# A state-space layer with its feed-forward block on eight cores: two kinds of diagonal weights sent through the weight ring, dt's row spread by DMA, one LayerNorm placed a stage earlier

## The reference

```python
xc, z = split(x @ W_in.T)                       # 2 x 2048 channels
xc = silu(causal_conv4(xc) + conv_b)            # each channel alone, 4 taps
dt, B, C = one, 16 and 16 rows of xc @ W_x.T
delta = softplus(dt * w_dt + b_dt)              # per channel
h_t = exp(delta_t * A) * h_(t-1) + delta_t * xc_t * B_t      # 16 states per channel
y = (sum over states of h_t * C_t) + D * xc
x1 = LayerNorm(x + (y * silu(z)) @ W_out.T)
h = gelu(x1 @ W1.T + scale * (rank-16 terms from 16 tokens) + b1)
x2 = LayerNorm(x1 + h @ W2.T + scale * (rank-16 terms) + b2)
```

## Time and profile before

| | |
|---|---|
| median of 3 runs | 3696.67 us (3695.38 to 3697.18) |
| the profiled execution | 3725.95 us |
| its span, core 3 (the slowest) | 3724.2 us |
| spans of the cores | 3678.0 to 3724.2 us |
| VectorE busy | 3136.2 us (84%) |
| TensorE busy | 3208.1 us (86%) |
| GpSimd busy | 1099.5 us (30%) |

### The profile page before, as it was taken

How to read it: one execution, slowest core, us unless ns; L and a number is a source line. 1 busy time by engine, 2 the same in 40 slices (tenths; PEclk the granted TensorE clock), 3 DMA queues, 4 the chain that set the end, 5 groups by cost and what they waited for, 6 DMA issues and landing times.

```text
span 3724.2 us, 72456 instructions; the slowest of 8 cores (3678.0 to 3724.2 us)
## 1 busy us (share of the span) xinstructions
PE 3208.1 (86%) x21816; PEld 2116.9 (57%) x21816; DVE 3136.2 (84%) x2688; ACT 2825.6 (76%) x4263; POOL 1099.5 (30%) x1541
## 2 busy tenths in 40 slices
PE   6666677988999889998999889998899879899998
PEld 2333344655666556655666556665566546666676
DVE  1999999988998999989988999999998899898400
ACT  4777768887797978878797977979788877977322
POOL 6222332224322143123323143332342242221312
PEclk9788888999999999999999989999999989988787
DMA  7466874435554444444554444544444435544565
GB/s 123 64 88 98 131 148 108 137 108 151 151 146 132 120 145 142 144 121 120 164 146 128 125 142 134 151 125 131 151 148 132 123 109 156 148 128 123 169 196 172
DMA packets 272053, 500.76 MB, mean 134 GB/s; under 512 B 28208, under 2 KB 67504, under 8 KB 270256
## 3 DMA queue, kind: packets, MB, share of 16 engines
q1 hardware_dynamic: 240320, 407.96, 37.2%
q0 software_dynamic: 14464, 71.26, 11.8%
q10 hardware_dynamic: 16896, 16.91, 1.3%
HBM read 533.59 MB, written 55.18 MB: 158 GB/s over the span
## 4 chain that ended last, share of the span: by engine, by line
PE 51%; DVE 21%; issue 13%; ACT 11%; POOL 2%; DMA 1%; DVEq 1%; ACTq 0%; SPq 0%; POOLq 0%
DVE hq L1030 14%; PE ps_f L696 8%; PE ps_dbx L546 8%; PE ps_f L732 8%; PE ps_y L562 8%; PE ps_f L574 7%; DVE hm L1040 6%; PE ps_f L638 4%; ACT da L876 3%; ACT L876 2%; PE ps_f L585 2%; PE ps_f L708 1%; ACT hh L935 1%; DVE xy L1047 1%; PE ps_f L719 1%
## 5 line engine op out<-in xcount | busy, mean ns | idle before, releaser
L1030 DVE TENSOR_TENSOR_SCAN hq<-da,state,ps_dbx 128x512 bf16<-128x512 f16 x1536 | 1856.5, 1261 | 216.6 <-PE ps_dbx L546 163.1
L876 ACT ACTIVATE da<-delta,prm_sb 128x512 f16<-128x512 f32 x2048 | 1363.0, 714 | 186.6 <-DVE hq L1030 128.1
L546 PE MATMUL ps_dbx<-dp,vt 128*128 128x256 bf16 x4096 | 649.5, 284 | 306.2 <-DVE hq L1030 303.0
L1030 DVE TENSOR_TENSOR_SCAN hq<-da,ps_dbx 128x512 bf16<-128x512 f16 x512 | 587.5, 1201 | 137.5 <-PE ps_dbx L546 121.9
L1040 DVE TENSOR_TENSOR hm<-hq,crep 128x2048 bf16<-128x2048 bf16 x512 | 698.4, 1364 | 2.3 <-PE ps_y L562 1.8
L546 PEld LDWEIGHTS ps_dbx<-dp,vt 128*128 128x128 bf16 x4096 | 385.7, 101 | 528.1 <-issue 428.1
L562 PE MATMUL ps_y<-hm,cst_sb 128*128 128x512 bf16 x2048 | 582.4, 411 | 0.7 <-DVE hm L1040 0.7
L1159 POOL CAST state<-hq 128x4 f32<-128x4 bf16 x384 | 71.8, 187 | 1701.1 <-DVE hm L1040 1696.4
L574 PE MATMUL ps_f<-xT,wr 128*128 128x512 bf16 x2048 | 498.7, 388 | 54.4 <-ACT hh L935 36.4
L696 PE MATMUL ps_f<-y,wr 128*128 128x256 bf16 x4096 | 515.8, 283 | 31.5 <-ACT hh L935 10.6
L732 PE MATMUL ps_f<-hh,wr 128*128 128x256 bf16 x4096 | 510.2, 281 | 2.1 <-ACT hh L935 1.4
(11 more groups left out here) (90 smaller groups left out, 2769.2 us busy)
## 6 DMA issues: line engine op xcount, KB each, us to landing
wr<-w_scr SPq DMA_DIRECT2D x1499, 256.0 KB, 2.9
w_scr<-wts POOLq DMA_DIRECT2D x28, 1024.0 KB, 11.9
crep<-c_scr POOLq DMA_DIRECT2D x32, 512.0 KB, 4.4
outT<-rr ACTq DMA_DIRECT2D x16, 1024.0 KB, 5.2
wr<-wts POOLq DMA_DIRECT2D x53, 256.0 KB, 5.6
xt_scr<-xt POOLq DMA_DIRECT2D x8, 1024.0 KB, 11.0
wr<-xt_scr SPq DMA_DIRECT2D x64, 128.0 KB, 3.1
xT<-xt_scr SPq DMA_DIRECT2D x48, 128.0 KB, 3.5
```

The costliest lines, as they stand in the source:

```text
L546: i = t.matmul(ps_dbx[s % 2][:, tb * 256:(tb + 1) * 256], vt[g % 2][:, tb * P:(tb + 1) * P], dp[:, k * 1024 + tb * 256:k * 1024 + (tb + 1) ...
L876: s_.activation(da[:, (e % NDA) * T:(e % NDA + 1) * T], delta[g % 2][:], AF.Exp, scale=a_col(dt, 2 * k + n)).then_inc(s_da, 1)
L1030: v.tensor_tensor_scan(hq[:, at:at + T], da[:, (e % NDA) * T:(e % NDA + 1) * T], ps_dbx[s % 2][:, n:2 * T:2], first, OP.mult, OP.add).then ...
```

## The change

The convolution's diagonals (for chunks from 2 on) and D's (for stages from 16 on) come from DRAM as weights in the ring, not from GpSimd. dt's row becomes row 33 of PR2's product; ScalarE copies it, writes it to DRAM and reads it back onto all partitions. PR2, PR3 and the store of C are placed two or three steps earlier. ST(c, 0, 2) is placed before the sixth pair of F1 items, not before the eighth: in 14.1 (chunks 1 and 5: 14.6). ST(c, 1, 1) is placed before the first F2 items (8.6 and not 9.1; chunks 1 and 5: 9.1 and not 9.4). After an ST in an even step, the second MUL comes in step s+6 and the store in s+8. `da` has 10 tiles, the ring of h 48 and not 52. Core of the diff:

```diff
-T_X, T_Z, T_WO, T_W1, T_W2, T_DT, N_TILES = 0, 16, 32, 48, 80, 112, 114
+T_X, T_Z, T_WO, T_W1, T_W2, T_CD, T_DD, N_TILES = 0, 16, 32, 48, 80, 112, 120, 122
-NDA = 9
+NDA = 10
-NH = 52
+NH = 48
@@ post_items
-    its += t2(c, 0) + d0[0][:2] + st(c, 1, 1) + d0[0][2:] + d0[1] + [("UT", c, 1)]
-    its += u1[0] + d0[2] + u1[1] + u1[2] + u1[3] + d0[3] + u1[4] + u1[5] + u1[6] + st(c, 0, 2) + u1[7]
+    its += t2(c, 0) + st(c, 1, 1) + d0[0] + d0[1] + [("UT", c, 1)]
+    its += u1[0] + d0[2] + u1[1] + u1[2] + u1[3] + d0[3] + u1[4] + [("GAP",)] + st(c, 0, 2)
+    its += u1[5] + u1[6] + u1[7]
@@ plan
-            pool[s1].append(("CD", c, j))
+            if c < 2:
+                pool[s1].append(("CD", c, j))
-        pe[b14 + 3].append(("PR1", c))
-        act[b14 + 4].append(("PR1", c))
-        pe[b14 + 4].append(("PR2", c))
-        act[b14 + 5].append(("PR2", c))
-        act[b14 + 6].append(("BNC", c))
-        pe[b14 + 6].append(("PR3", c))
-        act[b14 + 7].append(("PR3", c))
+        pe[b14 + 2].append(("PR2", c))
+        act[b14 + 3] += [("PR2", c), ("BNC", c)]
+        pe[b14 + 4].append(("PR3", c))
+        act[b14 + 5].append(("PR3", c))
+        act[b14 + 6].append(("DTREP", c))
-        pool[g * NP + 2].append(("DD", g))
+        if g < NDT:
+            pool[g * NP + 2].append(("DD", g))
+        else:
+            pe[g * NP + 6].insert(0, ("DD", g))
-                pool[s + 5].append(("MUL",) + it[1:] + (1,))
+                end = s + 5 if s % 2 == 1 else s + 6
+                pool[end].append(("MUL",) + it[1:] + (1,))
-                    act[s + 7].append(("STORE",) + it[1:3])
+                    act[end + 2].append(("STORE",) + it[1:3])
@@ sync_program (the SP queue)
+            if tile in cd_tiles or tile in dd_tiles:
+                src, at, n = (T_CD + tile[1] // 2, tile[1] % 2 * 512, 512) if tile in cd_tiles else \
+                    (T_DD + tile[1] // 8, tile[1] % 8 * P, P)
...
+                sy.dma_start(out=to[:, 0:n], in_=w_scr[src][:, at:at + n]).then_inc(s_wld[i % NW], 16)
@@ sum_states
+                if g < NDT:
...
+                else:
+                    t.matmul(ps_y[:], weights(("DD", g), 0)[:, 0:P], xy_tile(g),
+                             start=True, stop=False).then_inc(s_wused, 1)
@@ bc_rows
-                i = t.matmul(ps[0:32, :], cst[:, K_WX + k * 32:K_WX + (k + 1) * 32],
+                i = t.matmul(ps[0:33, :], cst[:, K_WX + k * 33:K_WX + (k + 1) * 33],
@@ bc_copy
+                s_.wait_ge(s_dtscr, 16 * c)
+            s_.copy(dtrow, ps[32:33, :]).then_inc(s_dtrow, 1)
@@ c_store
+            s_.wait_ge(s_dtrow, c + 1)
+            s_.dma_start(out=dt_scr[c % 2:c % 2 + 1], in_=dtrow).then_inc(s_dtscr, 16)
+        def dt_spread(c):
+            s_.wait_ge(s_dtscr, 16 * (c + 1))
+            if c > 0:
+                s_.wait_ge(s_edt, c * NDT)
+            s_.dma_start(out=dtrep[:], in_=dt_scr[c % 2].unsqueeze(0).broadcast_to([P, T])
+                         ).then_inc(s_dtrep, 16)
@@ delta_exp
-                s_.wait_ge(*emptied(("PR1", c)))
+                s_.wait_ge(s_dtrep, 16 * (c + 1))
```

More of the change, by code:

```diff
@@ L222, in place_casts @@
     pool[-40].append(("XFIRST", 1))
-    groups = [T_WO, T_WO + 4, T_X, T_Z, T_WO + 8, T_WO + 12, T_X + 4, T_Z + 4]
-    groups += [T_W1 + 4 * k for k in range(8)] + [T_X + 8, T_Z + 8, T_X + 12, T_Z + 12]
-    groups += [T_W2 + 4 * k for k in range(8)] + [T_DT]
+    groups = [T_WO, T_WO + 4, T_X, T_Z, T_CD, T_DD, T_WO + 8, T_WO + 12, T_X + 4, T_Z + 4]
+    groups += [T_W1 + 4 * k for k in range(8)] + [T_X + 8, T_Z + 8, T_X + 12, T_Z + 12, T_CD + 4]
+    groups += [T_W2 + 4 * k for k in range(8)]
     pool[2 * NP + 4].append(("XCAST", 0))
@@ L280, in tiles_of @@
         return [(T_Z + it[1] % NDT, True)]
-    if it[0] == "PR1":
-        return [(T_DT, False), (T_DT + 1, True)]
+    if it[0] == "X2" and it[1] >= 2:
+        return [(("CD", it[2]), True)]
+    if it[0] == "DD":
+        return [(("DD", it[1] % NDT), False)]
     if it[0] == "OUT":
@@ L446, in build_nc @@
     ps_f = [nc.alloc_psum_tensor(f"ps_f{j}", [P, 512], F32) for j in range(3)]
+    ut = rows[0:16, 0:TH]
+    dtrow = rows[32:33, :]
     ident = cst[:, K_ID:K_ID + P]
@@ L468, in sync_program @@
         cast_seen = set()
+        cd_tiles = [("CD", j) for j in range(NDT)]
+        dd_tiles = [("DD", j) for j in range(NDT)]
         x_after = {}
@@ L581, in conv @@
             ps = bank(it)
-            t.wait_ge(s_cd, n + 1)
+            if c < 2:
+                t.wait_ge(s_cd, n + 1)
+                diag = cdiag[n % 2]
+            else:
+                diag = weights(it, 0)
             t.wait_ge(s_halo, n + 1)
             for k in range(4):
-                i = t.matmul(ps[:], cdiag[n % 2][:, k * P:(k + 1) * P], xpre[n % 2][:, 1 + k:1 + k + T],
+                i = t.matmul(ps[:], diag[:, k * P:(k + 1) * P], xpre[n % 2][:, 1 + k:1 + k + T],
                              start=(k == 0), stop=(k == 3))
[L587 to L598, removed]
-                    i.then_inc(s_wused, 1)
             i.then_inc(full(it), 1)
@@ L825, in z_silu @@
             s_.activation(zs[:, (g % NZ) * T:(g % NZ + 1) * T], ps[:], AF.Silu).then_inc(free(it), 1)
-        def rows_copy(it):
-            s_.copy(dtrep[:], bank(it)[:]).then_inc(free(it), 1)
         def bc_copy(it):
@@ L915, in ut_copy @@
                 s_.wait_ge(s_su, 2 * c + h)
-            s_.copy(ut[:], ps[0:16, 0:TH]).then_inc(free(it), 1)
+            s_.copy(ut, ps[0:16, 0:TH]).then_inc(free(it), 1)
         def ltrow_copy(it):
@@ L994, in scalar_program @@
                     c_store(it[1])
+                elif it[0] == "DTREP":
+                    dt_spread(it[1])
                 elif it[0] == "STORE":
@@ L1297 @@
     wts[T_W1:T_W2] = f(L0_ffn_W1).reshape(32, P, NKD, P).transpose(0, 3, 2, 1)
-    wts[T_W2:T_DT] = f(L0_ffn_W2).reshape(8, P, 4, 8, P).transpose(0, 2, 4, 3, 1).reshape(32, P, 8, P)
+    wts[T_W2:T_CD] = f(L0_ffn_W2).reshape(8, P, 4, 8, P).transpose(0, 2, 4, 3, 1).reshape(32, P, 8, P)
     wx = f(L0_attn_W_x)
-    wts[T_DT:N_TILES] = wx[2 * NST].reshape(2, 8, P).transpose(0, 2, 1)[:, :, :, None]
+    lane = np.arange(P)
+    taps = f(L0_attn_conv_w).reshape(8, 2, P, 4)
+    for h in range(2):
+        for k in range(4):
+            wts[T_CD:T_DD, lane, h * 4 + k, lane] = taps[:, h, :, k]
+    for k in range(8):
+        wts[T_DD:N_TILES, lane, k, lane] = f(L0_attn_D_param).reshape(2, 8, P)[:, k]
     def cols(a, n):
```

37 lines of the change are left out of this document (22 added, 15 removed).

## The result

| | before | after |
|---|---|---|
| ratio of times, after to before | | 0.9907 (95%: 0.9878 to 0.9935) |
| the same, measured a second time | | 0.9892 (0.9855 to 0.9929) |
| the profiled execution | 3725.95 us | 3658.57 us |
| its span, slowest core | 3724.2 us | 3656.8 us |
| span of core 5 in it | 3679.8 us | 3647.5 us |

The change makes the kernel 0.9% faster: 0.9907 x 3696.67 = 3662 us, where 3640 was predicted. The ratios leave out executions in which half of the chip ran at a lower clock; with them the median after is 3685.41 us.

The account below looks back on a forecast made before the run. Neither VectorE (84% busy) nor TensorE (86%) was taken as a plain limit; the chain changes engines. Terms 56.5 - 16.6 + 4 + 4 + 15 - 5 - 1 = 57 us won gave 3669 profiled, median 3640 us, range 3600 to 3688.

Parts of the forecast that it names:

- second rival: Stage 14 takes most back through Z's wait, lower TensorE clock and late ScalarE: 10 to 40 us won, 3657 to 3687; chance 0.18.
- A, the crossings: Stage 15 and next chunk's stage 0: six with a LayerNorm fall from 61.15 us to 49.0 (four) and 57.2 (two), 56.5 won.
- B, stage 14: Z waits for the gelu PR1 hid, ST's matmuls added: 3.4 us in four chunks, 2 in two, 17.6 lost; chunk 0 may win 1.
- PEclk still 1.00: Expected profile sign: stage 14 at about 30 us with TensorE's clock figure unchanged at 1.00.
- C, GpSimd elsewhere: Outside the crossings: diagonals leave GpSimd's pairs, but ST(c, 1, 1) in 8.6 loses 8 us; net 4 won, bounds -8 to 20.
- D: SU in 10.2, behind DD, comes 0.6 us sooner in six or seven chunks: 4 us won, bounds 0 to 8.
- E, the tenth tile: `da` with 10 tiles lets ScalarE run one scan further ahead: 15 us won, bounds 0 and 48.
- waits for decays at 45 us: Expected profile sign: the scans' waits for decays, 59.7 us before, fall to 45 us.
- F, the ring: Weights' ring takes 232 places instead of 202, look-ahead shrinks 13%: 5 us lost, bounds 0 and 25.
- fourth rival: The ring becomes the bound, late small tiles holding up TensorE; at 1 us a stage 3752 us; chance 0.06.
- G, dt's path: DMA store and spread are hidden in chunks, up to 6 us each if uncovered; 1 us lost before the first scan, bounds 0 and 5.
- The rule on GpSimd and hm: hm makes no progress while GpSimd reads SBUF; the skill page's one-operation wait instead would make the crossings term 7 us better.

Follow-up runs that it names:

- a2: Kernel before with only the two LayerNorm STs moved, the steps of MUL and STORE, and the h ring of 48; ratio 0.9876 to the kernel before.
- c1: b3 with the ST of chunks 1 and 5 in 14.2 instead of 14.6; ratio 0.9850 to the kernel before.
- b1: Changed kernel with dt's row by PR1's 16 matmuls again and PR1, PR2, PR3 at their old steps; ratio 0.9856 to the kernel before.
- b3: Changed kernel with PR2 in 14.3, PR3 in 14.5, Z in 14.4, chunk 0's last copies to DRAM 18 steps later; ratio 0.9849 to the kernel before.
- c2: b3 with ST(c, 1, 1) back at its place in the kernel before; ratio 0.9824 to the kernel before.
- a4: Changed kernel with all diagonals built by GpSimd again and not in the ring; ratio 0.9931 to the kernel before.
- b2: Kernel before with only the ring of decays at 10 tiles, and the h ring of 48; ratio 1.0008 to the kernel before.
- a1: The changed kernel run once more; ratio 0.9892 to the kernel before.
- a3: Kernel before with only dt by DMA, PR2, PR3 and the store of C earlier, and the h ring of 48; ratio 1.0059 to the kernel before.
- b4: Kernel before with one wait more: GpSimd waits in 15.5 for the hm of 15.6; ratio 0.9986 to the kernel before.

## Why the prediction was right, and where its sizes were off

The direction and the place were right; 0.9% (35 us) came where 1.5% (57 us) was forecast, and 3662 us lies 5 us inside the second rival's numbers, whose mechanism, a lower TensorE clock in stage 14, is part of the answer.

- **A, the crossings: right.** 59.5 us won for 56.5. Four at 47.5 to 50.2 (49.0 forecast), two at 55.6 and 56.0 (57.2). a2 shows that the LayerNorm alone does it (54.7), c1 that what is left of the two long ones is the meeting with the DP items. The longest hm on core 5 is 3.88 us.
- **B, stage 14: mis-sized, 26.1 lost for 16.6.** The step that failed is "from 14.4, where PR2 stood with time to spare, nothing is won". Something is lost there: with PR2 in 14.2 beside an F1, products come 2.77 us late, and with 14.4 empty TensorE pauses 3.69 us and is, in most chunks, given the lower clock. The forecast 26.6 + 3.4 = 30.0 is what chunk 4 measured at 1.00, in part by luck: the scans' waits there (2.89 us for products behind PR2 and F1, 2.46 for a decay) are not those of the sum; at 0.90 it is 32.8. The sign "PEclk still 1.00" failed. Three chunks at 2.8 more and chunk 5, with 31.2 at 0.95 where 28.6 was forecast, make 11 us; chunk 0 gives 1.9 of it back. "ScalarE nothing" did not hold either: the scan of 14.4 waits 2.33 us for a decay, behind the gelu of the F1 that came late. Half of the loss, 11.5 to 13.3 us, is ST's own (a2, b1); the rest is placement, which b3 shows by taking 20.6 us back.
- **C, GpSimd elsewhere: right where it was tested.** 8 us were forecast lost by ST(c, 1, 1) in stage 9; a2 has 8.2 and c2 9.7 in stages 8 to 10. The diagonals win it back there (a4: 7 us), so stages 8 to 10 are unchanged in sum, 478.1 and 478.7.
- **D.** No run has it alone.
- **E, the tenth tile: wrong, nothing for 15.** b2 measured 1.0008. The sign "waits for decays at 45 us" failed too: they rose to 89.8. A wait for a decay isn't a full ring; I had put the price at a third of its bound without a row that showed ScalarE waiting for a free tile just before.
- **F, the ring: right in kind.** TensorE waited 16.2 us for tiles from DRAM (15.2 and, in F1, 1.0) and 13.8 before; a4 without the tiles has 9.1, b3 with them 13.9. It isn't the bound. One reading was wrong: of the five waits of the earlier trace rows two (7.8 us) lie at the start of chunk 1, the other three behind the last scan. The 32 KB loads land in 2.4 us where those of 256 KB take 3.0. The Trainium skill (DMA: Bandwidth & Descriptors, Specifications) puts the line rate at 512 bytes and more. The fourth rival's mechanism does occur, once in a core: TensorE waits for a D tile on cores 2 and 3 of the changed kernel (7.4 and 7.5 us), on three cores of a1 (3.2 to 5.2) and three of b1 (5.7 to 6.2), always in the first stages of chunk 1, where the other cores wait as long for tiles of 256 KB (11.5 us on core 5). So the queue was late there, and no run shows that the size of the loads cost anything.
- **G, dt's path: mis-sized.** At the start 1 us was forecast. Core 5 begins to scan at 80.7 to 85.0 us in the eight traces with this path and at 77.5 to 80.4 in the six without: some 4 us, where the ledger's one pair shows 7.1. The first crossing lost 8.7 where DMAs are in the way. The bound for a chunk without cover, 6 us, was too low, since it took landings from a quiet queue (1.5 to 4.4 us) for a stretch with 1024 KB copies, where one took 16.7. a3 puts the whole dt part at 0.59% slower: the step that I didn't take was to weigh the part by itself.
- The part of "all other stages" was forecast as 4 + 4 + 15 - 5 = 18 won and is 16.4, by luck: E is 0 in it. Which wait gave the rest stays open; these stages differ by as much between kernels that do nearly the same in them (b3 2770.8, c1 2785.0).
- **The rule on GpSimd and hm: half right.** "hm makes no progress while GpSimd reads SBUF" holds for the six longest hm of core 5 before (6.6 to 10.6 us) and not for others. In the stretch of the earlier trace rows the hm of 2.95 us, begun at 1753.06, waited for the end of one operation and went in ahead of V, which took 2.14 us and not 1.20; the hm of 10.62 us, begun at 1761.24, was passed over by all that followed:

```profile
1752.59 2.35 POOL L1185 TENSOR_TENSOR rr<-rr,stt 128x1024 f32<-128x1024 f32 x1
1754.88 2.14 POOL L1133 TENSOR_TENSOR vv<-delta,xy 128x512 bf16<-128x512 f32 x1
...
1759.47 2.36 POOL L1185 TENSOR_TENSOR rr<-rr,stt 128x1024 f32<-128x1024 f32 x1
```

In the six cases of core 5 where it was passed over, hm had begun 0.3 to 0.6 us before the running operation ended; in the nine where it had begun 0.7 to 2.2 us before, it entered behind that operation, although the next one followed without a gap. One more entered with 0.45 us left, ahead of a small copy. b4's hm of 5.83 and 5.32 us (0.6 and 0.5 us before) fit this. No experiment varied it, so what decides stays open. The Trainium skill (SBUF — State Buffer, Who interferes with whom) says of VectorE's two-port modes that whoever issues first holds the shared pair for the whole instruction, and of an operation with two SBUF inputs, such as hm, that it contends with GpSimd's reads. A wait of one instruction is what the cases that entered show, and the six long ones don't. By it the pause of b4 could shorten an hm by one operation of 2.36 us at most; it took 4.8 from one, and the work behind it put 4.1 on the next.

With the rest placed otherwise (b3) the ratio is 0.9849, with the losing move undone as well (c2) 0.9824: the change as made takes 0.9%, the same work at other places 1.5 to 1.8%.

## What to carry to other kernels

A change in several parts is worth a price for each part: here one part (two LayerNorms moved) gave 1.2%, one (diagonals by DMA) perhaps 0.3%, one (16 matmuls replaced by a DMA round trip) cost 0.6% and one (a tenth tile for the decays) nothing, and the whole read like a plain success. When an item leaves a step of a hand-written order, count TensorE's work per step on both sides: the emptied step can cost too, because the engine may be at the lower clock behind the pause (in five of six chunks here). Price a small DMA on a dependent path by the landing times of the stretch in which it will run, not by the median of the trace.
